# Graph kernel, third pass over the matrix: five piece buffers in place of four, shorter rings, and two groups interleaved where the second sweep meets the third

## The reference

```python
h = jnp.maximum(_layernorm(x), 0.0)
x = x + (adj.T @ h) / adj.sum(axis=0)[:, None]        # inf where the sum is 0 becomes 0
h = jnp.maximum(_layernorm(x), 0.0)
x1 = swish((adj @ h) @ W + b)
x2 = swish((adj @ x1) @ W + b)
return x + x2
```

## Time and profile before

| | us |
|---|---|
| median of 3 runs | 642.57 |
| lowest and highest | 640.7, 646.11 |
| the profiled execution | 648.0 |
| its span | 646.2 |
| PE busy | 615.4 (95%) |
| POOL busy | 543.6 (84%) |
| DVE busy | 539.3 (83%) |
| ACT busy | 318.0 (49%) |
| moved by DMA | 199.82 MB, mean 309 GB/s |

### The profile page before, as it was taken

One profiled execution on the slowest core, in us unless ns is written; L12 is line 12 of the kernel. 1 busy time (PEld: TensorE's weight loads), 2 busy tenths in 40 slices (PEclk: granted clock), 3 DMA queues, 4 the chain that ended last, 5 costly groups with the idle time before them and its releaser, 6 DMA issues.

```text
span 646.2 us, 6882 instructions
## 1 busy us (share of the span) xinstructions
PE 615.4 (95%) x2296; PEld 413.8 (64%) x2296; DVE 539.3 (83%) x558; ACT 318.0 (49%) x392; POOL 543.6 (84%) x277
## 2 busy tenths in 40 slices
PE   7889999999997999899999999999999999998796
PEld 5356666666564466567667667667677677676464
DVE  4988799878846999898888988998998988886694
ACT  2583442633532263755546447547546446445262
POOL 3299899599695479999989989998998999988593
PEclk9989999999999999999999999999999999999999
DMA  9999999999999999999999999829999999999971
GB/s 302 367 370 330 328 351 357 313 323 365 323 254 317 323 344 337 347 348 325 309 347 346 317 347 344 259 52 221 321 347 340 345 334 333 338 334 294 280 201 32
DMA packets 155828, 199.82 MB, mean 309 GB/s; under 512 B 5521, under 2 KB 138897, under 8 KB 155793
## 3 DMA queue, kind: packets, MB, share of 16 engines
q1 hardware_dynamic: 91568, 136.07, 67.0%
q10 hardware_dynamic: 64224, 63.32, 33.0%
HBM read 197.26 MB, written 2.10 MB: 309 GB/s over the span
## 4 chain that ended last, share of the span: by engine, by line
PE 38%; DMA 22%; POOL 22%; issue 7%; DVE 5%; ACTq 3%; ACT 2%; SPq 1%; POOLq 0%; DVEq 0%
DMA raw<-in_adj_dram 20%; POOL a_lo L837 11%; PE dg L439 10%; POOL at_lo L199 8%; PE dg L456 7%; PE dg L445 6%; PE dg L446 6%; PE m_ps L362 3%; ACTq L273 2%; DVE turned L726 2%; DMA h<-in_x_dram 2%; PE m_ps L469 1%; ACT at_hi L568 1%; PE m_ps L367 1%; PE m_ps L368 1%
## 5 line engine op out<-in xcount | busy, mean ns | idle before, releaser
L199 POOL TENSOR_TENSOR at_lo<-turned,at_hi 128x1024 fp32r<-128x1024 f32 x152 | 359.3, 2401 | 42.7 <-ACT at_hi L568 42.5
L726 DVE STREAM_TRANSPOSE turned<-raw 128x1024 f32<-128x1024 f32 x216 | 255.9, 1218 | 37.5 <-DMA raw<-in_adj_dram 32.8
L568 ACT ACTIVATE at_hi<-turned 128x1024 fp32r<-128x1024 f32 x152 | 155.6, 1054 | 123.1 <-DVE turned L726 65.6
L837 POOL TENSOR_TENSOR a_lo<-raw,a_hi 128x1024 fp32r<-128x1024 f32 x62 | 145.9, 2386 | 34.2 <-ACT a_hi L529 33.7
L681 DVE TENSOR_TENSOR dg<-raw,dg 128x2048 f32<-128x2048 f32 x60 | 137.5, 2292 | 37.7 <-DMA raw<-in_adj_dram 35.7
L445 PE MATMUL dg<-at_hi,f_hi 128*128 128x512 f32 x384 | 153.5, 400 | 7.9 <-ACT at_hi L568 7.9
L446 PE MATMUL dg<-at_hi,f_lo 128*128 128x512 f32 x384 | 151.5, 395 | 0.0
L456 PE MATMUL dg<-at_lo,f_hi 128*128 128x512 f32 x384 | 145.3, 460 | 3.9 <-POOL at_lo L199 2.4
L362 PE MATMUL m_ps<-raw,h 128*128 128x512 f32 x264 | 118.6, 594 | 5.4 <-DMA raw<-in_adj_dram 4.7
L439 PE MATMUL dg<-turned,f_w 128*128 128x512 f32 x256 | 120.3, 592 | 0.0
L456 PEld LDWEIGHTS dg<-at_lo,f_hi 128*128 128x128 f32 x384 | 71.8, 189 | 47.3 <-issue 28.4
(11 more groups left out here) (54 smaller groups left out, 311.6 us busy)
## 6 DMA issues: line engine op xcount, KB each, us to landing
raw<-in_adj_dram SPq DMA_DIRECT2D x64, 1024.0 KB, 7.6
raw<-in_adj_dram SPq DMA_DIRECT2D x120, 512.0 KB, 12.6
raw<-in_adj_dram ACTq DMA_DIRECT2D x120, 512.0 KB, 13.8
x<-in_x_dram SPq DMA_DIRECT2D x16, 128.0 KB, 8.2
out_dram<-zs SPq DMA_DIRECT2D x12, 128.0 KB, 14.7
h<-in_x_dram SPq DMA_DIRECT2D x1, 768.0 KB, 7.5
h<-in_x_dram SPq DMA_DIRECT2D x1, 256.0 KB, 2.8
out_dram<-zs SPq DMA_DIRECT2D x4, 64.0 KB, 1.9
```

Of the source, the lines that this page charges most:

```text
L199: return eng.tensor_tensor(at_lo[:, place(unit)], turned_tile(unit), at_hi[:, s % RING3].bitcast(f32), ALU.subtract)
L568: act.activation(at_hi[:, s % RING3], turned_tile(unit), ACT.Copy).then_inc(hi3_done, 1)
L726: dve.transpose(dst, src).then_inc(t3_done, 1)
L837: pool.tensor_tensor(a_lo[:, s % RING1], raw1[:, v % RAW1, i], a_hi[:, s % RING1].bitcast(f32), ALU.subtract).then_inc(lo1_done, 1)
```

## The change

It gives the pieces five buffers (`raw3_4` is new) and pays for them with memory: one buffer for `nT` and one for `zs` in place of two, `RING3` 3 for 4, `TURN` 8 for 9. Five pieces are kept between the sweeps (32 to 36). So that the last five pieces of sweep 2 are the first five of sweep 3, and none of the pieces of a group must be read before its factors are there, the last two groups of sweep 2 and the first two of sweep 3 are interleaved piece by piece: `TAIL2` and `HEAD3`.

```diff
-RAW3 = 4
-TURN = 9
-TURN_OFF = 4
+RAW3 = 5
+TURN = 8
+TURN_OFF = 3
 REST_LAG = 2
-RING3 = 4
+RING3 = 3
...
-PIECES = FIRST + tuple((n, q) for n in range(2, 2 * GROUPS) for q in range(QUARTERS))
+
+TAIL2 = ((6, 3), (7, 3), (6, 2), (7, 0), (6, 0), (7, 1), (6, 1), (7, 2))
+HEAD3 = tuple((n, q) for q in range(QUARTERS) for n in (GROUPS, GROUPS + 1))
+PIECES = (FIRST + tuple((n, q) for n in range(2, GROUPS - 2) for q in range(QUARTERS)) + TAIL2 + HEAD3
+          + tuple((n, q) for n in range(GROUPS + 2, 2 * GROUPS) for q in range(QUARTERS)))
...
-        raw3 = {3: sb("raw3_3", [P, GB, BC], into=sweep2)}
-        nT = sb("nT", [P, 2, QC], into=sweep2)
-        zs = sb("zs", [P, 2, QT, P], into=sweep2)
+        raw3 = {n: sb(f"raw3_{n}", [P, GB, BC], into=sweep2) for n in (3, 4)}
+        zs = sb("zs", [P, QT, P], into=sweep2)
+        nT = sb("nT", [P, QC], into=sweep2)
...
+            elif i == 4:
+
+                eng.wait_ge(main1_done, QUARTERS * PAIRS)
+                eng.wait_ge(deg_added, QUARTERS * PAIRS)
             elif i >= RAW3:
                 eng.wait_ge(t3_done, QU * (i - RAW3 + 1))
...
                 act.wait_ge(main3_done, last_unit(n) + 1)
-                act.wait_ge(rest3_done, split3(last_unit(n) - 1) + 1)
-                act.wait_ge(xw_done, r - 1) if r >= 2 else None
+                act.wait_ge(rest3_done, split3(last_split(n)) + 1)
+                act.wait_ge(xw_done, r) if r >= 1 else None
...
                 i = unit // QU + RAW3 - 1
                 if unit == 1:
                     load3(act, 3, ACT_BLOCKS)
+                    load3(act, 4, ACT_BLOCKS)
...
-                if 2 <= r < QUARTERS + 2:
-                    dve.wait_ge(x1_ready, r - 1)
-                elif r >= QUARTERS + 2:
-                    dve.wait_ge(y_out[r % 2], 16 * (P // SB))
+                if 1 <= r <= QUARTERS:
+                    dve.wait_ge(x1_ready, r)
+                elif r > QUARTERS:
+                    dve.wait_ge(y_out[(r - 1) % 2], 16 * (P // SB) * len(range(QUARTERS + (r - 1) % 2, r, 2)))
```

More of the change, by code:

```diff
@@ L107, in build @@
         f3_w = sb("f3_w", [P, UC * len(WHOLE3), P], into=sweep2)
-        raw3 = {3: sb("raw3_3", [P, GB, BC], into=sweep2)}
-        nT = sb("nT", [P, 2, QC], into=sweep2)
-        zs = sb("zs", [P, 2, QT, P], into=sweep2)
+        raw3 = {n: sb(f"raw3_{n}", [P, GB, BC], into=sweep2) for n in (3, 4)}
+        zs = sb("zs", [P, QT, P], into=sweep2)
+        nT = sb("nT", [P, QC], into=sweep2)
         w = sb("w", [P, P], into=sweep2)
         bias = sb("bias", [P, P], into=sweep2)
+        spare = sb("spare", [P, 256], into=sweep2)
         at_hi = sb("at_hi", [P, RING3, UC, GROUP], f32r, into=sweep2)
@@ L115, in build @@
             raw3[n] = sb(f"raw3_{n}", [P, GB, BC], into=sweep2)
-        spare = sb("spare", [P, 256], into=sweep2)
         turned = sb("turned", [P, TURN, UC, GROUP], into=whole_tiles)
@@ L216, in first_unit, with last_split, closing @@
             return min(QU * i for i in range(len(PIECES)) if PIECES[i][0] == n)
+        def last_split(n):
+            return max(unit for unit in splits3 if PIECES[unit // QU][0] == n)
+        def closing(n):
+            if last_split(n) + REST_LAG >= last_unit(n):
+                return last_split(n), True
+            return last_unit(n), False
         def piece_loads(i):
@@ L291, in store @@
             for b in blocks:
-                eng.dma_start(out_nodes[q, b][:, m], zs[b * SB:(b + 1) * SB, r % 2, m]).then_inc(y_out[r % 2], 16)
+                eng.dma_start(out_nodes[q, b][:, m], zs[b * SB:(b + 1) * SB, m]).then_inc(y_out[r % 2], 16)
         def turned_nodes(dst, half=None):
@@ L439, in main3 @@
                         mm = pe.matmul(acc, f_w[:, UC * WHOLE3.index(j) + c], turned[:, place(unit), c],
-                                       start=first and c == 0, stop=False)
+                                       start=first and c == 0, stop=closing(n) == (unit, False) and c == UC - 1)
                 else:
@@ L456, in rest3 @@
                     mm = pe.matmul(dg[:, 0, (n % 2) * 512:(n % 2 + 1) * 512], f_hi[:, r + c], at_lo[:, place(unit), c],
-                                   start=False, stop=unit + 1 == last_unit(n) and c == UC - 1)
+                                   start=False, stop=closing(n) == (unit, True) and c == UC - 1)
                 mm.then_inc(rest3_done, 1)
@@ L468, in xw @@
                     for m in range(QT)[tiles(r, part)]:
-                        mm = pe.matmul(m_ps[:, m * P:(m + 1) * P], nT[:, r % 2, m * P:(m + 1) * P], w[:, :],
+                        mm = pe.matmul(m_ps[:, m * P:(m + 1) * P], nT[:, m * P:(m + 1) * P], w[:, :],
                                        start=True, stop=True)
@@ L572, in copy_n @@
                 act.wait_ge(main3_done, last_unit(n) + 1)
-                act.wait_ge(rest3_done, split3(last_unit(n) - 1) + 1)
-                act.wait_ge(xw_done, r - 1) if r >= 2 else None
+                act.wait_ge(rest3_done, split3(last_split(n)) + 1)
+                act.wait_ge(xw_done, r) if r >= 1 else None
                 half = ORDER[n] % 2
-                act.activation(turned_nodes(nT[:, r % 2], half),
+                act.activation(turned_nodes(nT[:, :], half),
                                natural(dg[:, 0, (n % 2) * 512:(n % 2 + 1) * 512]), ACT.Copy).then_inc(n_copied, 1)
             def silu(r, part=0):
-                z = zs[:, r % 2, tiles(r, part)]
+                z = zs[:, tiles(r, part)]
                 act.wait_ge(z_ready, r + part + 1)
@@ L591, in x1_hi @@
                     at = UC * (WHOLE3 if j in WHOLE3 else SPLIT3).index(j)
-                    ins = act.activation(dst[:, at:at + UC], zs[:, r % 2, tiles], ACT.Copy)
+                    ins = act.activation(dst[:, at:at + UC], zs[:, tiles], ACT.Copy)
                 ins.then_inc(x1_split, 1)
@@ L732, in add_bias @@
                     dve.wait_ge(b_loaded, 16)
-                if 2 <= r < QUARTERS + 2:
-                    dve.wait_ge(x1_ready, r - 1)
-                elif r >= QUARTERS + 2:
-                    dve.wait_ge(y_out[r % 2], 16 * (P // SB))
-                dve.tensor_tensor(zs[:, r % 2, m], m_tiles(r, part),
+                if 1 <= r <= QUARTERS:
+                    dve.wait_ge(x1_ready, r)
+                elif r > QUARTERS:
+                    dve.wait_ge(y_out[(r - 1) % 2], 16 * (P // SB) * len(range(QUARTERS + (r - 1) % 2, r, 2)))
+                dve.tensor_tensor(zs[:, m], m_tiles(r, part),
                                   bias[:, :].rearrange("p (a d) -> p a d", a=1)
@@ L743, in residual @@
                 dve.wait_ge(silu_done, r + part + 1)
-                dve.tensor_tensor(zs[:, r % 2, m], m_tiles(r, part), x[:, q * QT:(q + 1) * QT][:, m], ALU.add)\
+                dve.tensor_tensor(zs[:, m], m_tiles(r, part), x[:, q * QT:(q + 1) * QT][:, m], ALU.add)\
                    .then_inc(y_ready, 1)
@@ L850, in lo_x1 @@
                     at = UC * SPLIT3.index(r * QU + mm)
-                    ins = pool.tensor_tensor(f3_lo[:, at:at + UC], zs[:, r % 2, UC * mm:UC * mm + UC],
+                    ins = pool.tensor_tensor(f3_lo[:, at:at + UC], zs[:, UC * mm:UC * mm + UC],
                                              f3_hi[:, at:at + UC].bitcast(f32), ALU.subtract)
```

## The result

| | before | after |
|---|---|---|
| median | 642.57 us | 653.08 us |
| lowest and highest | 640.7, 646.11 | 648.69, 654.22 |
| profiled execution, its span | 648.0, 646.2 | 648.69, 646.9 |

The ratio after to before is 1.0144, 95% interval 1.0107 to 1.0181: slower by 1.4%. The forecast was 643.5, within 1%; that was the likeliest case, and it did not come. The median lies just above the upper end of the range (653.0); by the ratio, 1.0144 x 642.57 = 651.8, the result lies inside. The ratios leave out executions over 1.5% above the fastest of their kernel.

What follows compares the result with a forecast made beforehand. PE, DMA and POOL were taken to limit the kernel together, with 7.1 us of idle PE from 592 us to win. Terms -6.0 + 5.0 + 1.0 + 1.0 gave +1.0 us: 643.6, called 643.5, range 634.5 to 653.

Steps and rivals of the forecast that it cites:

- Rival B: POOL runs dry once in every group, with ACT held and a ring of three: +9 us, 651.5; chance 0.22.
- Rival C: The fifth piece saves its load but DMA stays slow from 592 us on: +5 to +7, 648.5; chance 0.12.
- The fifth kept piece: End of sweep 3: four loads fewer, last piece lands one piece earlier, -6.0 us, capped by 7.1 us of idle PE.
- ACT issues each piece four units earlier: Sweep 2: ACT's issues hold it until a later piece lands, so POOL and PE start late: +5.0 us, bounds 0 and 7.6.
- with five buffers until piece p + 2 lands: Step of the ACT term: ACT held at unit 4p one piece longer than before, when piece p + 1 let it go.
- If at 435, the term of ACT is wrong: Test in the after profile: group 8's first matmuls at 439 to 441 us would support the ACT term.
- zs single: `add_bias` in sweep 3 waits only for `x1_ready` or a store 48 us earlier: 0, bounds 0 and +1 us.
- TURN 8: DVE eight units ahead of PE rather than nine, but DMA is what it waits for: 0, bounds 0 and +2 us.
- The ring of three: `at_hi` with three places: nothing in steady sweep 3, 0.35 us later three times where groups meet in sweep 2, +1.0 us.
- Interleaving: POOL's units come in a lump at the start of sweep 3 (HEAD3): +1.0 us, bounds 0 and 2.4.
- nT single: One buffer for nT: the `xw` that the copy waits for is as old as 48 us, so 0, bounds 0 and +1 us.
- Rival A: Issues stay cheap and the fifth buffer is simply worth a piece: -6.0 us, 637, capped at 635.5; chance 0.26.

Runs made afterwards that it cites:

- a_both: The changed kernel with the four stores of a pair issued together and ACT's loads issued four units later: 640.21 us, ratio 0.9968 to the kernel before.
- a_again: The changed kernel run once more, unchanged, for a second profile: 651.07 us, ratio 1.0123 to the kernel before.
- b_zs1: The kernel before with one buffer for zs and the waits that go with it: 650.1 us, ratio 1.0125.
- a_stores: The changed kernel with the four stores of a pair issued together by SP: 647.71 us, ratio 1.0064 to the kernel before.
- b_turn8: The kernel before with `turned` used over eight places, all else as before: 645.18 us, ratio 1.0055.
- b_inter: The kernel before, four buffers and four kept pieces, with only the interleaving of groups added, in a different piece order: 643.74 us, ratio 1.0013.
- a_actlate: The changed kernel with ACT's part of each load issued four units later, except piece 4: 643.28 us, ratio 1.0017 to the kernel before.
- a_both_p4: As a_both, with ACT's two blocks of piece 4 issued at unit 4 in place of unit 1: 639.81 us, ratio 0.9961 to the kernel before.
- a_spall: The changed kernel with stores together and SP issuing all four blocks of pieces 1 and up, ACT none: 829.53 us, ratio 1.2915 to the kernel before.

## Why the prediction was right or wrong

The sign of the sum was right and its size was not: +1.0 us forecast, and +9 measured (1.0144 of 642.57). Two terms were priced at nothing and cost 8 and 3.5 us when made alone; the fifth piece gave about what was forecast. The upper end of the range was set by rivals *B* and *C*, and neither is what happened, so it is in part luck that the range holds the result.

- **The fifth kept piece, -6.0.** Right in mechanism. Stage E loses its waits for data, by 5.9 to 8.6 us in a_both, depending on which profile with four pieces it is held against. DMA's loads were what DVE waited for there. The cap of 7.1 was read from idle PE alone, and one profile isn't enough to say that it was too low. By ratios, a_both less what TURN 8 costs is 0.9968 - 0.0055 = 0.991, -5.6 us for the piece and the interleaving together; this is a difference of two runs, not a run, with some 2.5 us to either side.
- **ACT issues each piece four units earlier, +5.0.** The size held and the place did not. Undone in the changed kernel it gives back 1.0144 - 1.0017 = 1.3%, some 8 us, though the interval of each ratio is 0.3 to 0.4% to either side, and the profiles show 4 to 6 us. But they lie in stage A, behind the start of sweep 2. In B, with the long holds of the earlier trace rows on which the term was built, nothing was lost: 149.0 against 149.7. The step that failed here is "with five buffers until piece p + 2 lands", and with it "POOL is worse off": the holds did not grow, they shrank. Of the seven issues of over 5 us in before, five lie in B; after has one in all, at 248.21 in A. From 292 to 440 us an issue of ACT took 1.01 us in the median and 5.2 at most before, and 0.51 and 3.8 after. So POOL is idle ahead of `lo3` only 2.0 us more than before, where 5 to 10 were forecast, and over the whole span the median issue is 0.51 us after and 0.52 before, where over 1 was forecast. Why the holds shrank is open.
- **The test for it was badly put.** "If at 435, the term of ACT is wrong" was an absolute time. By PE's timeline group 8 began at 434.62 before and at 435.52 after, 0.9 later; but sweep 2 had also begun 2.4 earlier. From its start, group 8 comes after 204.4 us before, 207.7 after and 209.8 in a_again (440.51 - 230.73): delays of 3.3 and 5.4 us, near the forecast 5.0, but from A.
- **zs single: 0, bounds 0 and +1.** This is the step that failed worst: "`add_bias` of a pair waits for `x1_ready` or the store of the pair before, 48 us earlier". That is true of the work, and not of the stores. The first of the four is issued 31 us before DVE wants the buffer (559.72 against 590.3), the last only 8 us before, because SP spreads them one to a piece, and it needs 15 us to land. Alone it costs 1.25% (b_zs1), with stores together it is gone (a_stores, -0.8%). I had looked up the wait and not the event that ends it; the rows of SP's stores stood in the trace of before.
- **TURN 8: 0, bounds 0 and +2.** Measured +0.55%, 3.5 us. "what it waits for is DMA" wasn't enough: DVE's waits for PE rose from 4.5 to 22.7 us in b_turn8. That each of these also delays the freeing of a piece's buffer, and so the loads, is my reading; no run separates it.
- **The ring of three, +1.0.** Nothing, as far as the error tells (1.0007, so -1.5 to +2.5 us). ACT waits more for POOL, where it had time.
- **Interleaving, +1.0, bounds 0 and 2.4.** Alone, in its other order, +0.8 us (-1.4 to +3.0). In stage C the changed kernel loses 2.0 us and b_inter 0.5. Of the former, 1.1 us are idle time of PE: 0.7 waiting for POOL, 0.4 for ACT. POOL is busy for 24.00 of 24 us from 456 to 480, but it was so before as well. The lump of POOL's work fits this and isn't shown by it, and the other 0.9 us isn't placed. a_both has the same 50.8, so neither repair touches it.
- **nT single** wasn't tried alone. D is 97.0 in every kernel with it but a_stores (97.7), so it costs nothing there that shows.

*Rival B* came out in size (+9) and not in kind: POOL doesn't run dry once in each group, and the ring that it blames is free in the kernel before. *Rival A* is refuted as to the holds, which cost what a_actlate gives back, though the piece is worth about what A claimed. *Rival C*, that the end keeps its slow data, is refuted by 347 GB/s in a_both.

The losses aren't simply added: b_zs1, b_turn8 and ACT's early place come to 1.25 + 0.55 + 1.3 = 3.1%, less 0.9% for the piece 2.2%, where 1.4% is measured. One reason shows: b_zs1 waits for stores 7.3 us in D and 7.8 in E, after only 1.2 in D and 7.5 in E. The rest is open. From the changed kernel, the two repairs do add up within their error: 1.0064 + 1.0017 - 1.0144 = 0.994 against 0.997 measured.

The best version is a_both (or a_both_p4): the change with the stores together and ACT's loads four units later beats the kernel before by 0.3 to 0.4%. The gain left is small; the shorter ring of `turned`, which pays for the fifth piece with others, cost 0.55% when made alone.

## What to carry to other kernels

When a double buffer becomes single, find the last event that frees it and when it is issued, not how old its work is: here four stores had been spread over the very time that the second buffer gave. A deeper ring asks for the issue of its loads to be placed anew, since an engine that both computes and issues stands still for as long as an issue takes, up to 5.2 us here. And compare stages by distances between fixed points of the work, not by times from the start of the span.

## What the runs showed of the hardware

- A stall of PE can cost nearly twice its length. In after, 3.44 us of idle PE were followed by a granted clock of 0.52 and 0.63 over 8 us, 2.8 us more. The two waits for stores in b_zs1 were followed by 0.79 (548 to 556 us) and 0.57 (604 to 612). The stretch behind 592 us of before, with six idle pieces of at most 1.58 us each to 626 us, kept 1.00 and paid only for its idle time. The length of one wait doesn't decide alone: 1.92 us in after, the last of four waits in 14 us, was followed by 0.57 from 248 to 252 us, and 2.44 us in a_again by 0.69 from 240 to 244; but 2.24 us in a_again (253.05) and 1.97 us in before (267.17) kept 1.00.
- One queue doesn't carry the full rate with every kind of load. In a_spall, SP's queue alone moves sweep 2 at 212 GB/s; SP's and ACT's together move the same 512 KB blocks at 338 to 347. But in sweep 1 of before, SP's queue alone moves 338 GB/s from 60 to 150 us. Its loads are of 1 MB there, and its packets of 3.1 KB in the mean (30.33 MB in 9687), against 1.0 KB in a_spall (30.42 MB in 30626, from 288 to 432 us). No run tells which of these it is. The Trainium skill (DMA: Bandwidth & Descriptors, Issuing engines are not separate DMA queues) says that initiating DMAs on several engines at once saves only the time that the sequencer needs for it. For the blocks of sweep 2 these runs disagree, by a factor of 1.6: SP's issues took 2.35 us in the median in a_spall, but the shortest took 0.31.
- A DMA issue can hold its engine: three issues took 6.57 us of ACT in a_again. That the queue was full then is my reading. The same section's "usually small relative to the DMA itself" holds for the median (0.51 us against 13.0 from issue to landing) and not for these.
- A store of 128 KB takes 14.7 us in the median from issue to landing when the stores go out one at a time between the loads (before, after), so a buffer behind a store comes free late. Issued four together it takes 10.0 (a_stores) and 11.4 (a_both), and 8.6 in a_spall, where they are together too and the loads come at 212 GB/s.
